# Output projection, gate and sum moved into the attention steps of a gated attention and feed-forward block

## The reference

```python
xn = layernorm(x)                       # by row, no weights
# s: causal attention, 16 heads of 16
q, k, v = split(xn @ w_qkv); q = q / 4
attn = softmax(mask(q @ k^T))           # 4 batches x 16 heads, 1024 x 1024
s = (attn @ v) @ w_out
# f: six feed-forward blocks, 256 -> 1024 -> 256
for i in range(6):
    f = gelu(f @ W1[i].T + B1[i]) @ W2[i].T + B2[i] + f
    if i < 5: f = layernorm(f) * LN_G[i] + LN_B[i]
out = x + s * silu(f)                   # silu(f) = f * sigmoid(f) = 0.5 * f * (1 + tanh(f / 2))
```

## Time and profile before

| what | value |
|---|---|
| median of three executions | 1761.65 us (1760.46 to 1762.91) |
| the profiled execution's own time | 1765.19 us |
| its span, first to last instruction | 1763.5 us |
| granted TensorE clock, mean over the span | 0.972 |
| PE, DVE, ACT, POOL busy in the span | 94%, 65%, 49%, 17% |
| `mlp` ends, `attend` starts | at about 1354 us |
| last `values` matmul of `attend` ends | at about 1662.5 us |
| first matmul of `combine` | at about 1689.7 us |

### The profile page before, as it was taken

The page is one execution under the profiler, slowest core; times in us unless marked ns, Lnnn a source line. Parts: engine busy times, 40 slices in busy tenths (PEclk is TensorE's granted clock), DMA queues, the critical chain, the costliest instruction groups (busy, mean ns, idle before and its releaser), DMA issues. The chain is left out here.

```text
span 1763.5 us, 29499 instructions
## 1 busy us (share of the span) xinstructions
PE 1656.3 (94%) x11216; PEld 1345.9 (76%) x11216; DVE 1149.4 (65%) x2924; ACT 870.6 (49%) x1220; POOL 305.8 (17%) x290
## 2 busy tenths in 40 slices
PE   6989999999999999999999999999998998899656
PEld 5879888888888888898888888889986443334246
DVE  7736776787877777778776777765554554454045
ACT  3444443444444444444443444344444998899522
POOL 1031111111111111111111111111102232223113
PEclk9989999999999999999999999999998999999868
DMA  8859334251020201202021020220302455533324
GB/s 279 300 179 210 84 86 92 83 121 50 16 50 13 43 13 26 39 13 49 14 43 23 10 46 13 37 76 1 62 1 60 115 155 128 147 101 94 97 94 157
DMA packets 73033, 141.88 MB, mean 80 GB/s; under 512 B 9984, under 2 KB 49408, under 8 KB 66112
## 3 DMA queue, kind: packets, MB, share of 16 engines
q1 hardware_dynamic: 72896, 140.05, 30.0%
HBM read 109.34 MB, written 55.84 MB: 94 GB/s over the span
## 5 line engine op out<-in xcount | busy, mean ns | idle before, releaser
L616 ACT ACTIVATE m_hid<-m_h_ps,m_b1s 128x512 f32<-128x512 f32 x384 | 264.7, 689 | 718.5 <-PE m_h_ps L714 696.4
L677 DVE TENSOR_TENSOR m_hidl<-m_hid,m_hidh 128x512 fp32r<-128x512 f32 x384 | 279.9, 729 | 269.4 <-ACT m_hidh L619 268.7
L867 ACT ACTIVATE a_prob<-a_st_ps 128x1024 f32<-128x1024 f32 x288 | 277.6, 1022 | 28.3 <-PE a_st_ps L905 22.9
L727 PE MATMUL m_y_ps<-shared,m_hidh 128*128 128x256 f32 x1536 | 284.5, 283 | 0.0
L714 PE MATMUL m_h_ps<-m_xth,shared 128*128 128x512 f32 x768 | 276.2, 401 | 6.3 <-issue 4.0
L592 POOL TENSOR_TENSOR xres<-xres,m_b2s 128x1024 f32<-128x1024 f32 x48 | 132.7, 2766 | 756.2 <-DVE xres L633 756.2
L619 ACT ACTIVATE m_hidh<-m_h_ps,m_b1s 128x512 fp32r<-128x512 f32 x384 | 260.7, 679 | 0.0
L727 PEld LDWEIGHTS m_y_ps<-shared,m_hidh 128*128 128x128 f32 x1536 | 248.1, 189 | 14.8
L727 PE MATMUL m_y_ps<-w2h,m_hidh 128*128 128x256 f32 x768 | 216.7, 282 | 0.0
L727 PE MATMUL m_y_ps<-shared,m_hidl 128*128 128x256 f32 x768 | 215.8, 281 | 0.0
L727 PE MATMUL m_y_ps<-w2l,m_hidh 128*128 128x256 f32 x768 | 214.0, 279 | 0.0
(11 more groups left out here) (114 smaller groups left out, 2713.9 us busy)
## 6 DMA issues: line engine op xcount, KB each, us to landing
shared<-q_stacks SPq DMA_DIRECT2D x32, 400.0 KB
shared<-k_stacks SPq DMA_DIRECT2D x32, 400.0 KB
q_stacks<-q_parts SPq DMA_DIRECT2D x96, 128.0 KB
k_stacks<-k_parts SPq DMA_DIRECT2D x96, 128.0 KB
mk<-k_stacks SPq DMA_DIRECT2D x32, 384.0 KB, 10.7
q_parts<-mq SPq DMA_DIRECT2D x16, 512.0 KB, 4.2
k_parts<-mk SPq DMA_DIRECT2D x16, 512.0 KB, 3.6
mq<-q_stacks SPq DMA_DIRECT2D x21, 384.0 KB, 4.9
```

The costliest lines, as they stand in the source:

```text
L616: nc.scalar.activation(hid[n % 2][:], h_ps[n % 2][:], ACT.Gelu, bias=b1s[i % 2][:, k:k + 1])
L677: nc.vector.tensor_tensor(hidl[n % 4][:], hid[n % 2][:], hidh[n % 4][:].bitcast(F32), ALU.subtract).then_inc(low_done, 1)
L727: m = nc.tensor.matmul(y_ps[:, j, :], h[n % 4][:, j * P:(j + 1) * P], w[par][:, k, :], start=(k == 0 and j % 2 == 0 and h is hidh and w is ...
L867: nc.scalar.activation(to, scores, ACT.Exp).then_inc(exp_done, 1)
```

## The change

There is no `combine` block. Its work is done inside `attend`, which now runs on for 15 steps after the last group.

- **Denominators.** `copy_o` now writes one buffer per half. SP moves it on by `move` (line 867/869 of the kernel after): per half four DMAs of 16x512 values into `num`, where two groups make 128 partitions, and four of one row of 512 denominators into DRAM. For each pair of groups and each half there follow `gather` (875: the 8 x 512 denominators come back as 128x32), `invert` on DVE (996, 128x32), `keep` (879: to DRAM), `spread` (886: eight DMAs, each one row of 512 inverses to 16 partitions), `divide` on DVE (1000, 128x512), `high` on POOL (the high part, 128x512) and `low` on DVE (1004, 128x512). `DELAYS` says how many steps after the copy each stands; for the last group `LAST_DELAYS`.
- **Projection.** `project_tile` on PE (1088): six matmuls per tile of 128 rows straight from `onh`/`onl`, without transposes, into a part of `s_ps`, the buffer of the search; DVE multiplies by the gate (`mix`, 1013), POOL adds `x`, SP stores. The 32 tiles stand at steps 45 to 59 (batch 0), 81 to 95 (batch 1), 117 to 131 (batch 2) and 147 to 155 (batch 3).
- **Gate.** `0.5 * f * (1 + tanh(f/2))`: the `Tanh` (ACT, 128x1024) and the multiplication (DVE, `SCALAR_TENSOR_TENSOR` 128x1024) of a slot stand in the slot behind it in the last feed-forward block, chunks 4 and 5; the last slot's at steps 18 and 20 of the attention.
- `store_o`, the transposes, the 32 `Silu` and the block boundary go.

```diff
@@ mlp, ScalarE and VectorE
+            def half_tanh(t):
+                act.wait_ge(b2_added, t + 1)
...
+                nc.scalar.activation(keep["tanh"], xx, ACT.Tanh, scale=0.5).then_inc(tanh_done, 1)
...
+                if k == 4 and t > LAST:
+                    half_tanh(t - 1)
...
                 if t >= NORMED:
+                    if k == 5:
+                        dve.wait_ge(tanh_done, t - LAST + 1)
+                        nc.vector.scalar_tensor_tensor(xx, keep["tanh"], 1.0, xx, ALU.add, ALU.mult).then_inc(gated, 1)
                     return
@@ attend
+DELAYS = {"move": 1, "gather": 3, "invert": 5, "keep": 5, "spread": 7, "divide": 9, "high": 9, "low": 11}
+LAST_DELAYS = {"move": 1, "gather": 2, "invert": 3, "keep": 3, "spread": 4, "divide": 5, "high": 5, "low": 6}
+def part_copied_at(n, half):
+    return NS * n + LAST_STEP[half] + LATE
...
+            if n % HG == HG - 1:
+                for j in range(TILES):
+                    tiles.setdefault(at + (7 + j if last else 13 + 3 * half + 2 * j), []).append(QT * (n // HG) + TILES * half + j)
@@ SyncE
-            def store_o(n):
-                bt, hg = divmod(n, HG)
-                sp.wait_ge(o_copied, 2 * n + 2)
+            def move(n, half):
+                sp.wait_ge(o_copied, 2 * n + half + 1)
...
                 for j in range(HG):
-                    sp.dma_start(od[hg, j, :, SEQ * bt:SEQ * (bt + 1)],
-                                 oout[n % 2][2 * HD * j:2 * HD * j + HD + 1, :]).then_inc(o_stored[n % 2], 16)
+                    to = slice(HG * HD * (n % 2) + HD * j, HG * HD * (n % 2) + HD * (j + 1))
+                    sp.dma_start(num[n // 2 % 2][half][to, :], oout[half][2 * HD * j:2 * HD * j + HD, :]).then_inc(moved[half], 16)
+                    row = 2 * HD * j + HD
+                    sp.dma_start(scratch["den"][n // 2, half, HG * (n % 2) + j:HG * (n % 2) + j + 1, :], oout[half][row:row + 1, :]).then_inc(den_stored[half], 16)
+            def gather(n, half):
+                sp.wait_ge(den_stored[half], 16 * HG * (n + 1))
...
+            def keep_inverse(n, half):
+                sp.wait_ge(inverted, n // 2 * 2 + half + 1)
...
+            def spread(n, half):
+                sp.wait_ge(inv_stored[half], 16 * (n // 2 + 1))
...
+                for h in range(2 * HG):
+                    sp.dma_start(den[half][HD * h:HD * (h + 1), :], scratch["inv"][n // 2, half, h:h + 1, :].broadcast_to([HD, BANK])).then_inc(inv_loaded[half], 16)
@@ VectorE
+                if stage == "invert":
+                    dve.wait_ge(flat_loaded[half], 16 * nth)
...
+                elif stage == "divide":
+                    dve.wait_ge(moved[half], 16 * HG * (n + 1))
+                    dve.wait_ge(inv_loaded[half], 16 * 2 * HG * nth)
@@ TensorE
+            def project_tile(i, seen):
+                half, j = i % QT // TILES, i % TILES
+                if j == 0:
+                    pe.wait_ge(normed, HG * (i // QT) + HG - 1 + half)
...
+                pe.wait_ge(search.maxed, 2 * seen)
+                if i >= 2:
+                    pe.wait_ge(mixed, i - 1)
+                for c in range(HALVES):
+                    for t, w in ((onh, woh), (onh, wol), (onl, woh)):
+                        m = nc.tensor.matmul(s_ps[:, i % 2, 0:DIM], t[half][:, c, P * j:P * (j + 1)], w[:, c, :],
...
                 for v in AT.get(at, ()):
+                    if projected:
+                        pe.wait_ge(mixed, projected)
                     search.pe_visit(pe, s_ps, v, False)
+                    seen = v + 1
+                for i in TILES_AT.get(at, ()):
+                    project_tile(i, seen)
+                    projected = i + 1
```

More of the change, by code:

```diff
@@ L36 @@
 LOADS = 4
-OUT_DMAS = HG
-OT = 4
+FLAT = 2 * HG * BANK // P
+TILE_BUFS = 4
 NEG = -1.0e30
@@ L809, in _, with store @@
+            def store(i):
+                c = i % TILE_BUFS
+                sp.wait_ge(added, i + 1)
+                sp.dma_start(out[P * i:P * (i + 1), :], res[c][:]).then_inc(stored[c], 16)
+            sp.dma_start(wo_raw[:], wout.rearrange("(c p) n -> p c n", p=P)).then_inc(wo_loaded, 16)
+            for i in range(TILE_BUFS):
+                load_x(i)
             load_values(sp, scratch, keep, 1)
-            for at in range(ALL):
+            for at in range(END):
                 n, step = divmod(at, NS)
@@ L828, in _ @@
                         load_values(sp, scratch, keep, bt)
[L829 to L832, removed]
-                load_pair(sp, x, od, keep, 2 * c, c)
-            store_o(N_GROUPS - 1)
-            for u in range(2):
-                sp.wait_ge(o_stored[u], 16 * OUT_DMAS * (N_GROUPS // 2))
+                for n, half, stage in STAGES_AT.get(at, ()):
+                    if stage == "move":
+                        move(n, half)
+                    if stage == "gather":
+                        gather(n, half)
+                    if stage == "keep":
+                        keep_inverse(n, half)
+                    if stage == "spread":
+                        spread(n, half)
+                for i in TILES_AT.get(at - 2, ()):
+                    store(i)
+                    if i + TILE_BUFS < N_TILES:
+                        load_x(i + TILE_BUFS)
+            for c in range(TILE_BUFS):
+                sp.wait_ge(stored[c], 16 * (N_TILES // TILE_BUFS))
         @block.gpsimd
         def _(pool):
-            for at in range(ALL):
+            for at in range(END):
                 n, step = divmod(at, NS)
-                for i, col in enumerate(DIAGONALS[step]):
+                for i, col in enumerate(DIAGONALS[step] if at < ALL else ()):
                     if i == 0:
@@ L1144, in gated_block @@
             mlp(nc, w1t, w2t, b1, b2, ln_g, ln_b, scratch, keep, search)
[L1145 to L1154 removed]
+        attend(nc, x, wout, out, scratch, keep, search)
 def kernel(L0_attn_x, L0_attn_w_qkv, L0_attn_w_out, L0_ffn_W1, L0_ffn_B1, L0_ffn_W2, L0_ffn_B2, L0_ffn_LN_G, L0_ffn_LN_B):
```

288 lines of the change are left out of this document (124 added, 164 removed).

## The result

The changed kernel takes 1787.24 us (median of four runs, 1779.52 to 1790.35) against 1761.82 us of the kernel before on the same chip: ratio 1.0129, 95% interval 1.0111 to 1.0148. It is slower; 1747 was forecast. The profiled execution took 1786.62 us with a span of 1784.9.

A forecast was written before the change was run, and what follows sets the result against it. It took TensorE and ScalarE as full in the attention, with 101.0 us behind it where no engine is full. -75.7 + 42 + 7 + 26 - 15 + 1 = -14.7 from 1765.2 gave 1750.5, 1747 on the median's scale; range 1706 to 1795.

The forecast's parts named there:

- Tail: Behind the last attention matmul: 101.0 us of stores, block change and combine give way to a 25.3 us chain, -75.7 us.
- The projection in the steps: 24 tiles in the attention's steps: TensorE waits for VectorE's reduction in 18, 2.2 us each, 0.4 in six others; +42 us.
- the clock: In the attention, one TensorE pause in four at the tiles brings its clock to the low level, 1.5 us each: +7 us.
- The chain of the denominators: Beside the attention: VectorE waits for late inverses at the divides, TensorE loses part of that; +26 us with 1 for clock.
- What the attention gets back: In the attention: without the 17-row stores on one DMA engine, stacks come less late; -15 us of 21.7 lost.
- The gate: Seven Tanh hidden in the feed-forward block, the eighth on a full ScalarE in the attention: +1 us.
- C: Rival: in the attention small transfers wait behind loads, TensorE held 5 us each half, nothing comes back; 1806 us, chance 0.14.
- B: Rival: pauses at the tiles of batches 1 to 3 keep TensorE at 1.2 GHz, 54 us for 7; 1794 us, chance 0.12.
- A: Rival: the projection in the attention is nearly free and the clock holds, 10 us for 49; 1708 us, chance 0.12.
- D: Rival: the denominators' waits in the attention are all hidden and the whole 20 us come back; 1716 us, chance 0.12.

The follow-up runs named there:

- run 1: The changed kernel without the denominators' trip (no gather, reciprocal, store of the inverses or spread): 1718.7 us, ratio 0.9754 to the kernel before.
- run 2: The changed kernel with the first 24 tiles left out, with their product, sum, loads and stores: 1744.86 us, ratio 0.9907 to the kernel before.
- run 6: The changed kernel with one transfer of four rows in place of four and one spread in place of eight, same bytes: 1763.96 us, ratio 1.0014.
- run 7: The changed kernel with the attention's loads of stacks, for scores and search, cut to one row of each side, issues kept: 1764.33 us, ratio 1.0008.
- run 9: The kernel before with each store of 17 rows split into one of 16 rows and one of 1: 1725.78 us, ratio 0.9801.
- run 14: The changed kernel without the gate's tanh and product in the feed-forward stage (six of eight pieces left out): 1790.29 us, ratio 1.0166.
- run 13: The changed kernel with later stages, tiles ahead of the visit, fewer issues and rows stored first, without the first 24 tiles: 1695.28 us, ratio 0.9621.
- run 5: The changed kernel with the denominators' stages further apart (divide 15 steps behind the copy instead of 9) and tiles later: 1753.32 us, ratio 0.9946.

## Why the prediction was wrong

The sign was wrong. What stood in the sum for -14.7 came out at +21.4 between the two spans (1763.5 and 1784.9). By its own steps:

- **Tail**: 25.3 us forecast, 28.6 came. The failed piece is the price of an issue. The four stores of the earlier trace rows cost 0.30 each, but a move costs 0.51 and a row store 0.44, with gaps 1.04 a pair and 4.1 us a half against 2.4, and a spread 3.5 against 2.4. +3.3.
- **The projection in the steps**: 42 and 7 for the clock forecast, 62.6 came, +13.6. The mechanism was right: 17 of the 18 tiles behind a visit paused, 1.1 to 1.6 us, and the usual pair of steps with such a tile is 2.1 us longer, forecast 2.2; a pair with a tile and no visit is 0.4 longer, as forecast. That makes 40 of the 62.6. The term that was too small is the clock. The other 22 us lie in pairs of steps in which the granted clock was at its low level for a part. Nearly half of them are at steps 45, 47 and 81 (pairs 6.0, 4.5 and 3.9 us longer), where the stall at a divide had just brought the clock down and the low part and the divide come late as well; the rest are at 87, 95, 117 and 121 to 126. Around the first two:

```profile
1440.00:1476.00 36.00, 29.40 (x200) 13.08 (x204) 15.89 (x35) 21.04 (x22) 8.57 (x14) 0.77 0.48 138
```

- **The chain of the denominators**: 26 us forecast, 50.6 came in the steps, +24.6, beside the 12 that run 1 finds in the tail; without tiles to hide under it would be 71 (run 2). **This is the step that turned the sign.** The list by groups had the right places, and even the longest wait, 11.6 us at step 79 where 10 near 77 was said: its 6, 4.5, 2.5, 8, 2.5, 1.5 and 0 are 12, 5, 6, 13, 6, 6 and 3 in the trace. It was too small for four reasons, the first two of which runs 6 and 7 take apart: SyncE's issues cost 1.7 times what was taken; a store of inverses was given 1.9 us and had 4.2 in the median, since a store behind 1.5 MB of loads lands behind them; and SyncE stands still meanwhile, which delays the next half. TensorE also lost nearly all that VectorE waited (8.80 of 9.39), not half of it: at step 30 it had come to the next visit 2.7 us behind VectorE. The fourth reason is again the clock, given 1 us: a pause of that length left it at its low level, and step 31 behind it takes 3.5 us on a TensorE that is busy throughout:

```profile
1424.93:1428.44 3.51, 3.51 (x20) 0.97 (x24) 0.42 (x1) 1.95 (x3) 0.00 (x0) 0.50 0.66 175
```

  The first step behind each of the stalls at 43, 66, 79, 102 and 115 takes 3.5 to 3.7 us too. Added up over the one or two steps behind each stall that is some 12 of the 50.6 us, an estimate from the starts of the exponentials.
- **What the attention gets back**: 15 forecast. The attention grew by 97.1 = 50.6 + 62.6 + 1 (gate) less 17.1, and run 9, which takes away the transfers of 17 rows alone, gives 16.9. The rule of the Trainium skill named there ("DMA: Bandwidth & Descriptors", "Why a DMA increments its semaphore by 16 and not by 1") gives 16 rows sixteen engines and 17 rows one; run 9 agrees with it: with 16 rows to a transfer the values land in 12.8 us instead of 24.9. The 21.7 us that the prediction set beside it were too many, since some 5 of them are no stall of the loads: run 9 keeps 291.4 us, not 286.4. The same cause held 20 us of the tail, which the prediction counted among the gains of the change without seeing that one line would have brought them.
- **The gate**: +1 forecast. Step 18, with the eighth `Tanh`, takes 3.0 us instead of 2.1; the other seven show nothing that can be measured (run 14).

3.3 + 13.6 + 24.6, less 3.6 for the earlier start and 2.1 for what came back, are 35.8: the distance from -14.7 to +21.4, but for 0.3.

The rivals: C (1806) had the mechanism, the queue, but it tied two things together that come apart: the chain was late and the 15 us came back all the same. B's time, 1794, is the nearest to 1787, and its mechanism took a part. Its mark was a clock under 0.8 in the steps with tiles, the forecast's one near 1.00; it was 0.88, 0.88 and 0.83 in the three stretches. It was not kept low: behind the tiles of steps 45 and 47 it was at its high level with tiles and pauses going on:

```profile
1480.00:1510.00 30.00, 24.35 (x211) 12.31 (x211) 13.97 (x45) 19.60 (x21) 10.46 (x17) 1.00 0.68 148
```

What it costs shows in steps 117 to 131, in the changed kernel and in run 14, which has the same attention: 46.8 us and 39.7 for the same work.

```profile
1679.40:1726.20 46.80, 42.81 (x313) 19.84 (x316) 16.54 (x37) 29.65 (x32) 16.71 (x25) 0.83 0.45 118
```

```profile
1680.50:1720.20 39.70, 35.73 (x313) 17.85 (x309) 16.52 (x37) 29.49 (x31) 16.76 (x25) 1.00 0.51 136
```

A (1708) and D (1716) are out: the tiles' pauses and VectorE's waits at the divides, 55.1 us, were paid. The tail stayed under the 32 us that the forecast had set as its mark; the attention grew by 97, past its mark of 95.

Not settled: why 27 us of the chain remain in run 13 with the divide 16 steps behind the copy, and whether an order of SyncE's queue exists that hides it wholly.

## What to carry to other kernels

A wait added to an engine that works in order costs what stands behind it. Give a chain of small transfers through memory as many steps as its worst landing, not its median, and count each issue of its queue at its own measured price. Put new work on TensorE ahead of the matmuls whose reduction it would otherwise wait for; together with fewer issues these turned 1.3% slower into 2.6% faster. Price a pause of TensorE with the slower steps behind it: at step 31 that was 1.5 us more. And when a change removes a slow transfer, first make that transfer fast in the kernel as it is: here that alone gave 38 us, where the best of the rebuilt kernels gave 47.

## What the runs showed of the hardware

- The price of an issue on SyncE depends on the transfer: 0.30 us for 17 rows to DRAM, 0.51 for 16 rows from SBUF to SBUF, 0.43 for one row, 0.44 for a spread. One transfer that spreads eight rows costs 0.64 to 0.68 to issue (run 6), where the eight took 3.54.
- A store of 16 KB landed in 1.4 us in the median where the loads' bytes were taken away (run 7), and in up to 14.7 us behind 2.5 MB of search loads and values from the same queue (run 5, line 879):

```profile
DMA to landing us min/median/max: 1.4/1.7/14.7
```

- Splitting 17 rows into 16 and 1 took 128 issues instead of 64 and made the kernel before 2.0% faster (run 9).
- After the 8.80 us in which TensorE stood at step 30 its granted clock was 0.50 (1.2 GHz) over step 31, and the step took 3.51 us on a busy TensorE instead of 1.99.
